# Building the first stack of heads on TensorE instead of loading it back from DRAM, with later projections moved

## The reference

```python
q = split_heads(x @ Wq)
k = split_heads(x @ Wk)
v = split_heads(x @ Wv)
attn = jnp.einsum('bhqd,bhkd->bhqk', q, k) * scale
attn = jax.nn.softmax(attn, axis=-1)
attn = attn + bias[None]
out = jnp.einsum('bhqk,bhkd->bhqd', attn, v)
# layer norm, residual, layer norm, then:
sim = jnp.einsum('btp,np->btn', x @ hasher_w.T, keys)
vals, idx = jax.lax.top_k(sim, 4)
# the four chosen experts: silu(x @ down) @ up, weighted by softmax(vals)
```

## Time and profile before

| | |
|---|---|
| three executions | 300.12, 297.38 and 299.98 us, median 299.98 us |
| the profiled execution | 298.97 us, of it 297.1 us span |
| busy: PE, DVE, ACT, POOL | 93%, 81%, 65%, 41% of the span |
| first score of round 0 | 37.59 us after the span's start |

### The profile page before, as it was taken

The page is one execution under the profiler, slowest core; times in us unless marked ns, Lnnn a source line. Parts: engine busy times, 40 slices in busy tenths (PEclk is TensorE's granted clock), DMA queues, the critical chain, the costliest instruction groups (busy, mean ns, idle before and its releaser), DMA issues.

```text
span 297.1 us, 10991 instructions
## 1 busy us (share of the span) xinstructions
PE 277.7 (93%) x4661; PEld 147.8 (50%) x4661; DVE 240.7 (81%) x525; ACT 194.2 (65%) x382; POOL 121.2 (41%) x210
## 2 busy tenths in 40 slices
PE   4959999999999999999999999999999999989992
PEld 3545434444444344445557554445565645467482
DVE  4857989998999989987787799987877866668854
ACT  3652388776777677689864876988556589831720
POOL 8486134110104742127556412089375034014852
PEclk9998999999999999999999999999999999999998
DMA  5567067255042302000502030005200000100011
GB/s 161 157 158 168 2 152 129 66 146 154 2 106 61 82 4 84 4 2 15 150 6 82 3 82 5 3 3 155 47 4 2 6 3 2 39 2 2 2 38 36
DMA packets 18575, 17.28 MB, mean 58 GB/s; under 512 B 6830, under 2 KB 16222, under 8 KB 18526
## 3 DMA queue, kind: packets, MB, share of 16 engines
q1 hardware_dynamic: 17856, 16.39, 22.1%
q10 hardware_dynamic: 670, 0.19, 0.3%
HBM read 12.18 MB, written 4.23 MB: 55 GB/s over the span
## 4 chain that ended last, share of the span: by engine, by line
PE 75%; DVE 11%; DMA 6%; POOL 3%; issue 2%; SPq 1%; ACT 1%; POOLq 0%; DVEq 0%
PE sm_ps L1275 16%; PE st_ps L1275 15%; PE ov_ps L1330 15%; PE si_ps L1275 8%; PE mi_ps L1275 7%; DVE neg_max L956 6%; DMA k_stack<-parts_dram 3%; PE mi_ps L1337 1%; PE si_ps L1355 1%; PE st_ps L1587 1%; PE sm_ps L1355 1%; PE st_ps L1461 1%; DMA x_sb<-L_attn_x 1%; PE st_ps L1502 1%; DVE parts L940 1%
## 5 line engine op out<-in xcount | busy, mean ns | idle before, releaser
L956 DVE TENSOR_REDUCE neg_max<-sm_ps 128x1 f32<-128x512 f32 x256 | 166.2, 685 | 29.1 <-PE sm_ps L1275 24.0
L808 ACT ACTIVATE probs<-st_ps 128x512 f32<-128x512 f32 x256 | 137.1, 603 | 34.7 <-PE st_ps L1275 34.4
L1275 PE MATMUL sm_ps<-k_stack,q_stack 96*32 96x512 bf16 x984 | 97.4, 383 | 3.1 <-DVE neg_max L956 2.5
L1275 PE MATMUL st_ps<-q_stack,k_stack 128*32 128x512 bf16 x1024 | 88.9, 380 | 0.3 <-ACT probs L808 0.2
L1330 PE MATMUL ov_ps<-probs,v_cur 128*32 128x256 f32 x1024 | 76.5, 378 | 0.0
L1275 PEld LDWEIGHTS sm_ps<-k_stack,q_stack 96*32 96x32 bf16 x984 | 26.4, 94 | 50.3 <-DVE neg_max L956 33.6
L1330 PEld LDWEIGHTS ov_ps<-probs,v_cur 128*32 128x32 f32 x1024 | 32.0, 110 | 22.2
L1275 PEld LDWEIGHTS st_ps<-q_stack,k_stack 128*32 128x32 bf16 x1024 | 27.9, 96 | 27.3 <-ACT probs L808 8.0
L534 POOL TENSOR_TENSOR hid<-hid,w_rows 128x512 f32<-128x512 f32 x19 | 24.1, 1281 | 21.6 <-ACT w_rows L710 21.6
L1275 PE MATMUL mi_ps<-x_t,down_sb 128*32 128x512 f32 x192 | 25.2, 593 | 0.0
L1275 PE MATMUL si_ps<-up_sb,hid 128*32 128x128 f32 x768 | 24.2, 273 | 0.0
(11 more groups left out here) (190 smaller groups left out, 303.1 us busy)
## 6 DMA issues: line engine op xcount, KB each, us to landing
q_stack<-parts_dram SPq DMA_DIRECT2D x16, 288.0 KB
k_stack<-parts_dram SPq DMA_DIRECT2D x48, 96.0 KB
parts_dram<-parts SPq DMA_DIRECT2D x24, 128.0 KB, 2.4
x_sb<-L_attn_x SPq DMA_DIRECT2D x4, 256.0 KB, 4.4
out<-y_out SPq DMA_DIRECT2D x3, 256.0 KB, 2.6
down_sb<-L_ffn_values_down SPq DMA_DIRECT2D x1, 512.0 KB, 5.8
up_sb<-L_ffn_values_up SPq DMA_DIRECT2D x1, 512.0 KB, 8.0
rel_win<-rel_dram SPq DMA_DIRECT2D x1, 256.0 KB, 2.9
```

The lines of the kernel that those rows point to most:

```text
L808: nc.scalar.activation(probs[:, u % 2, j, :], st_ps[:, score_bank(u * J + j), :], ACT.Exp, scale=SCORE_SCALE).then_inc(probs_ready, 1)
L956: nc.vector.tensor_reduce(neg_max[:, g % 2, col:col + 1], sm_ps[:, c % 2, :], AX.X, ALU.max, negate=True).then_inc(max_ready, 1)
L1275: i = nc.tensor.matmul(dst[n * TILE:(n + 1) * TILE], weights[:, n * TILE:(n + 1) * TILE], moving, **flags)
```

## The change

Stack 0 of batch 0 no longer goes through DRAM. POOL makes two matrices of zeros and ones, `pick_q` and `pick_k` (six more POOL instructions). PE multiplies the bf16 parts by them: `queries_stack(j)` is one tile group of 3 tiles, `keys_stack(j)` three such groups that add up, for each head j of 0 to 3; each group writes the rows 0 to 95 of a PSUM bank in the order that the stack needs, and ACT copies these into `q_stack` and `k_stack` (`stack_copy`, 8 in all). The first 16 maxima wait for these copies, the later ones for the loads as before. Each load of stack 0 for batch 1 has one more transfer in front (24 zero rows of `q_stack`, copied from stack 1). Around it:

- batch 2's queries and keys are made at the preparation's end, where batch 3's were, and batch 3's in round 0, at the end of the units 1 and 3; with them go ACT's copies (`late_parts`, `middle_parts`) and POOL's residues and low parts;
- the turn of x for batch 3 moves behind the values of batches 0 and 1; the turned x and the values use other banks;
- batch 1's residues and the values' copies of batches 2 and 3 on DVE move between the maxima 6 to 9;
- POOL adds beta to batch 0 only after batch 0's low parts (`first_split`);
- the turn of the first shift is in tiles and stands in the middle of the last bias product, with 4 of its 8 pieces behind it, and ACT copies it ahead of the last bias copy.

```diff
+        pick_q = sb("pick_q", [P, J, TILE], BF16)
+        pick_k = sb("pick_k", [P, PARTS, J, TILE], BF16)
...
-            return [st_ps[:, 0, :], ov_ps[:, :], sm_ps[:, 0, :], sm_ps[:, 1, :]][b]
+            return [st_ps[:, 0, :], ov_ps[:, :], mi_ps[:, :], si_ps[:, :]][b]
...
-            return [st_ps[:, 0, :], ov_ps[:, :]][b % 2]
+            return [st_ps[:, 0, :], si_ps[:, :], st_ps[:, 2, :], si_ps[:, :]][b]
+
+        def stack_bank(j, a):
+
+            return [(st_ps[:, 1, :], st_ps[:, 2, :]), (ov_ps[:, :], st_ps[:, 0, :])][j % 2][a]
...
+                if t == 1 and g == 0:
+                    sp.dma_start(q_stack[TERMS:SHIFT_ROW, 0:J, :], q_stack[TERMS:SHIFT_ROW, J:2 * J, :]) \
+                      .then_inc(stack_loaded[g], 16)
...
+            nc.gpsimd.memset(pick_q[:], 0.0)
+            nc.gpsimd.memset(pick_k[:], 0.0).then_inc(picks_made, 1)
+            pool.wait_ge(picks_made, 1)
...
             pool.wait_ge(beta_loaded, 16)
+            pool.wait_ge(first_split, 2)
             add_beta(0)
...
+            act.wait_ge(stack_set, 1)
+            act.wait_ge(rows_cleared, 1)
+            stack_copy(0, 0)
+            stack_copy(0, 1)
             x_copy(2)
+            stack_copy(1, 0)
+            stack_copy(1, 1)
+            stack_copy(2, 0)
+            stack_copy(2, 1)
             x_copy(3)
-            high_parts(1)
+            high_part(1, 0)
+            stack_copy(3, 0)
+            stack_copy(3, 1)
+            high_part(1, 1)
             middle_parts(1)
...
                     if u == 0 and is0(t):
-                        last_parts(0)
-                    if u == 3 and is0(t):
-                        middle_parts(B - 1)
+                        late_parts(2, 0)
+                    if u in (3, 4) and is0(t):
+                        late_parts(3, 4 - u)
+                    if u == 7 and is0(t):
+                        middle_parts(3)
+                    if u == 2 and is0(t):
+                        middle_parts(2)
...
+            def queries_stack(j):
+
+                for i in range(PARTS):
+                    n = nc.tensor.matmul(stack_bank(j, 0)[i * TILE:(i + 1) * TILE], pick_q[:, j, :], parts[:, 0, 0, i, :],
+                                         start=True, stop=True)
+                n.then_inc(stack_made, 1)
+
+            def keys_stack(j, terms=range(PARTS)):
+
+                for k in terms:
+                    for i in range(PARTS):
+                        n = nc.tensor.matmul(stack_bank(j, 1)[i * TILE:(i + 1) * TILE], pick_k[:, k, j, :],
+                                             parts[:, 0, 1, k, :], start=(k == 0), stop=(k == PARTS - 1))
...
             for kc in range(C):
                 for piece in range(2):
                     bias_product(G - 1, kc, piece, 2)
-                    early_maxima(1, product=tiled)
-            early_maxima(EARLY, J * C + 2, tiled)
-            pe.wait_ge(table_copied, 3)
-            make_qk(B - 1, 1)
-            early_maxima(1, EARLY)
-            pe.wait_ge(consts_made, 8)
-            pe.wait_ge(shift_split, 1)
-            turn(mi_bf[:, 0:P], shift_parts[:].rearrange("p i n -> p (i n)"), ident_bf[:]).then_inc(misc_ready, 1)
+                    early_maxima(1, EARLY, tiled)
+                if kc == 1:
+                    pe.wait_ge(consts_made, 8)
+                    pe.wait_ge(shift_split, 1)
+                    tiled_turn(mi_bf[:, 0:P], shift_parts[:].rearrange("p i n -> p (i n)"), ident_bf[:]) \
+                        .then_inc(misc_ready, 1)
...
+                    if is0(t) and u == 1:
+                        pe.wait_ge(last_copied, late_count(2, 1))
+                        make_qk(3, 1)
+                    if is0(t) and u == 3:
+                        pe.wait_ge(misc_done, job(0, "shift1", is_kept))
+                        make_qk(3, 0)
```

More of the change, by code:

```diff
@@ L428, in _ @@
             sp.wait_ge(first_written[0], PARTS * 16)
-            load_queries(0, 0)
+            load_queries(0, 1)
             sp.wait_ge(first_written[1], PARTS * 16)
-            load_keys(0, 0)
-            for g in range(1, G):
+            load_keys(0, 1)
+            for g in range(2, G):
                 load_slice(0, g)
@@ L621, in round_ @@
                 if is0(t):
-                    low_parts(B - 1)
+                    low_parts(2)
                 if experts:
@@ new lines, in _ @@
+            queries_stack(0)
+            pe.wait_ge(resid_made, 2)
+            pe.wait_ge(first_mid, 2)
+            keys_stack(0, range(PARTS - 1))
+            pe.wait_ge(first_split, 2)
+            keys_stack(0, range(PARTS - 1, PARTS))
+            queries_stack(1)
+            early_maxima(2, product=tiled)
+            pe.wait_ge(v_copied, 1)
+            keys_stack(1)
+            pe.wait_ge(v_copied, 2)
+            turn_x(3)
+            early_maxima(1)
+            pe.wait_ge(stack_copied, 2)
@@ new lines, in _ @@
+            queries_stack(2)
+            keys_stack(2)
+            early_maxima(1)
+            pe.wait_ge(xt_copied, 3)
+            make_qk(1, 0)
+            early_maxima(1)
+            pe.wait_ge(stack_copied, 4)
+            queries_stack(3)
+            keys_stack(3)
+            early_maxima(1)
+            pe.wait_ge(stack_copied, 5)
+            make_qk(1, 1)
+            early_maxima(1)
+            pe.wait_ge(stack_copied, 6)
+            make_v(2)
+            early_maxima(1)
+            make_v(3)
@@ L1485, in _ @@
+            early_maxima(1)
+            pe.wait_ge(stack_copied, 8)
+            early_maxima(1)
+            pe.wait_ge(high_made, 3)
+            pe.wait_ge(resid_made, 3)
             pe.wait_ge(rel_loaded, 16)
```

118 lines of the change are left out of this document (69 added, 49 removed).

## The result

| | before | after |
|---|---|---|
| median of 20 executions each | 298.86 us | 301.85 us |
| lowest to highest | 296.90 to 300.51 us | 299.61 to 302.97 us |
| ratio, with its 95% interval | | 1.0101 (1.0078 to 1.0124) |
| span of the profiled execution | 297.1 us | 300.4 us |

The changed kernel is 1.0% slower, 3.0 us. The profiled executions differ by 3.3 us of span (3.25 unrounded).

What follows compares the result with a forecast made beforehand. PE was taken as the bound of the preparation, DVE's maxima pacing part, and PE and DVE both full in round 0. Preparation -0.9 and round 0 +1.2 us gave +0.3 on 298.97: 299.3 us, range 296.6 to 302.0 us.

Steps and rivals of the forecast that it cites:

- the values of unit 5: Sign in round 0: the values of unit 5 come 0.3 us later than before, near 53.8 us.
- the first score: Sign at round 0's start: first score near 36.5 us; prediction wrong if ahead of 35 us or behind 38.
- the waits for exponentials: Sign in round 0: prediction wrong if PE waits for exponentials in units 3 to 5 by over 0.5 us together.
- The start: Preparation: first maximum at 13.0 us instead of 20.92, low parts 0.55 us each, stack groups 0.22 us, longest wait 1.5 us.
- products run one after another: Rival, preparation: tiles run one after another, stack costs 6.2 us instead of 3.5; +2.7 us, 302.0 us; chance 0.04.
- low parts stay slow: Part of a rival, preparation: low parts stay at 1.4 us or more, +1.2 us; chance 0.08 shared with the clock's return.
- The low clock: Preparation: half clock behind the wait for stack 0 leaves, saving 1.7 us, as the longest gap left is 1.5 us.
- the third rival: Start gains less: low parts stay slow or 0.5 clock returns among small gaps; +1.2 or +1.7 us, 300.5 to 301.0; chance 0.08.
- Round 0 pays: Round 0: two projections, 1.72 us, moved in at the ends of units 1 and 3 cost 1.2 us, bounds 0.6 and 1.72.
- the room that I let PE use afterwards: Round 0: PE has 0.25 us of room in each of four five-maxima units behind the first projection, 1.0 us in all.
- ScalarE becomes the bound: Rival, units 2 to 4 of round 0: six more ACT copies uncovered cost +2.9 us, 302.2 us; chance 0.14.
- Loads "0": Loads of stacks 1 to 3 move up, and the 24 zero rows add one transfer; both were to cost 0.

Runs made afterwards that it cites:

- second trace: Both kernels run unchanged once more, for a second trace of each; the kernel before took 297.65 us this time.
- G: Changed kernel with both batch 3 projections moved from round 0 into the gap at the keys table, ScalarE's copies behind it: 298.11 us, ratio 0.9987 to the kernel before.
- D: Changed kernel with batch 3's two projections in round 0 over 128 of their 512 columns only: 299.73 us, ratio 1.0057 to the kernel before.
- E: Changed kernel with batch 3's two projections in round 0 as four tiles side by side instead of one whole product: 301.47 us, ratio 1.0123 to the kernel before.
- F: As E, but the keys' projection cut into four pieces of 128 columns, at the ends of units 1 to 4: 300.61 us, ratio 1.0052 to the kernel before.

## Why the prediction was wrong

Forecast 299.3 us, measured 301.85, so no change was forecast where 1.0% was lost. The measured time is still under the 302.0 us that the range ended at, but by luck: that end stood for ScalarE's copies as the bound, which cost 0.19 us. A loss of more than 1% had a chance of 0.16. Of the signs named, the values of unit 5 came at 56.27 us for 53.8 and the clock did fall ahead of 60 us; the first score (37.78) and the waits for exponentials (0.28 us) stayed inside their bounds, since neither looks at the time that round 0 lost to DVE. In the order of its steps:

- **The start: right.** First maximum at 13.21 us for 13.0. The low parts take 1.47 us for the two, 0.7 each for 0.55. A stack group takes 0.22 us. A tiled group behind a whole one starts 0.31 us later (14.90 to 15.21), so 0.1 us a change. The longest wait is 1.50 us at the keys table for 1.5. The rivals "products run one after another" and "low parts stay slow" are out.
- **"The low clock ... 1.7 us. It leaves if no gap of that size is left": the step that failed in the preparation.** It stood again, 3.4 us long, behind a gap half as long, the very 1.5 us that the prediction had found and thought harmless. That is the third rival, to which I gave 0.08, though it looked for the cause among small gaps. The first score came at 37.78 us; with the 1.7 us out it would be at 36.1, ahead of the forecast near 36.5. All other terms together were thus right to about half a microsecond. Without the clock's term the sum said that the preparation gets 0.8 to 1.05 us longer; up to the first score it got 0.19 us longer.
- Nor was the other side of that term safe. The kernel before does not always pay it: 2.41 us of waiting left the clock at 1.00 in its second trace. I had one trace, and made a property of the kernel out of one execution.
- **"Round 0 pays ... I take 1.2 us": the second step that failed, and the largest part of what the change costs.** It was 2.33 us (0.42 at u1 to 2.75 at u4), above my upper bound of 1.72. Three things: the room that I let PE use afterwards, which took the 1.72 down to 1.2 and was not there; the two changes between tiled and whole products at each projection, 0.4 us together, a price which stood in my own sum for the preparation and which I left out here; and 0.19 us for ScalarE. Together 1.1 us. The error on the room was one of reasoning: the text says that DVE is as full as PE, and then lets PE catch up. Here it never did: the offset stays at 2.75 to 2.76 us from u4 to u15, and the 1.07 us that DVE stands idle are lost. I had also let two banks hold 1.2 us of maxima; DVE's idle time (1.07 and 1.08) equals PE's absence (1.05 and 1.06), so there was no such lead.
- **ScalarE becomes the bound: no.** The copies cost 0.19 us, the wait of 0.28 us in unit 3, not 2.9. G shows the same step without batch 3's late copies, so it comes with the two of unit 2.
- **Loads "0": not in this trace.** The wait for stack 3 of batch 1 cost 0.89 us more in the profiled execution than in that of before. In the second trace of the changed kernel it cost 0.20 us less than in that of before, so most of the 0.89 is variation of the landing; a part of the change in it is neither shown nor ruled out. That this transfer stood in the chain of the kernel before I could have read.
- **The sum** for the profiled execution: 0.44 (preparation) + 2.31 (round 0, u0 to u15) + 0.89 (round 1) - 0.02 (from there to the last exponential) - 0.37 (behind it, not looked into) = 3.25 us, the difference of the spans. Against the forecast's +0.3 that is 2.95 us too much: 1.34 from the preparation (+0.44 for -0.9), 1.11 from round 0 (2.31 for 1.2), 0.89 from round 1, less 0.39 for the rest. For the medians the last three terms have no claim, and the mean of the clock differs too: at a mean clock from 0.990 to 0.994 the spans are 296.5 and 300.1 us, 3.6 apart; the medians of all executions are 3.0 apart, as the mix of clocks differs.

What stays open: why a gap of 1.50 us is followed by half clock in five traces (both of the changed kernel, D, E and F) and not in a sixth (the version without POOL's wait), and one of 2.41 us not either. Ahead of PE's last product the traces show falls behind these five gaps and the one of 3.23 us alone; none came behind a wait of 1.02 us or less.

## What to carry to other kernels

Before moving work into a stretch where two engines are full, ask which engine will stand idle meanwhile: its idle time is the price, and room on the other doesn't give it back. Put moved work where PE waits anyway; filling a wait of 1.5 us with 1.7 us of products freed 2.3 us elsewhere and held the clock. Before a low clock is entered as a saving, look whether it is there in every execution: the mean clock of each run tells, once the fall at the program's end is allowed for.

## What the runs showed of the hardware that I had not expected

- The granted clock fell to 0.50 for about 3.4 us behind a gap of 1.50 us, in both traces of the changed kernel and in three of its variants, and did not behind the same gap in another, nor behind 2.41 us. The Trainium skill (TensorE: Matmul & The Clock Gate, "Why this matters for your kernels") warns of gaps over about 3 us; the falls behind 3.23 and none behind 2.41 us fit it, the five behind 1.50 us do not, and the traces decide.
- In E, four tiles in fp32 side by side cost as much as one whole fp32 product (0.86 us for 512 columns), and between other tiled products they save the changes, 0.2 us.
- The landing of one transfer of the same size, at the same place of the same program, varied by at least 1.1 us between two executions.
